# Rope attention on one core: q, k and their projections as three products of rounded operands and rests

## The chip, the cores and the metric

The kernel runs on one core of one Trainium2 chip. The metric is the device time in microseconds of one execution. Before the change it is 2147.18 us, the median of three runs (2139.17 to 2151.58).

## The reference

A stack of four layers works on 2048 tokens of 128 channels; each layer is an attention (or a recurrence) and a feed-forward part, each followed by a norm. Two places matter here. Both are causal attentions with rotary embedding over 4 sequences of 512 tokens:

- the attention of layer 2: 8 heads of 128 channels (the scores are q·k of 128 terms),
- the attention inside the feed-forward part of layer 2: 16 heads of 64 channels, with biases on q, k and v.

For each head: q = x·Wq, k = x·Wk, both rotated (`even*cos - odd*sin`, `even*sin + odd*cos`), scores = q·k with a causal mask, a softmax over the keys, the product with v, and the output projection, summed over the heads. All of it is float32.

## The kernel before

Both attentions are built by one function, `rope_attention`. The first call is named a2 (`heads=1`; in the profile its tiles begin with `a_`), the second h2 (`heads=2`; tiles begin with `h_`). Activations lie with channels on the 128 partitions and tokens along the free dimension.

The work is cut into 32 units U: 4 sequences b times 8 groups g. A unit of a2 is one head of 128 channels, a unit of h2 two heads of 64 channels, which lie on the upper and lower 64 partitions (`rows`). Each unit has four steps n = 0 to 3, one for each tile of 128 queries, in the order of query tiles 3, 0, 2, 1; a step's scores are as wide as its keys reach, so the four steps are 512, 128, 384 and 256 columns wide. In this document S512, S128, S384 and S256 are the score products of these steps (line 1210), T0 to T3 the transposes of the steps' probabilities (line 1220).

Each engine runs its own program, written out by hand, in order, and the engines wait for each other by semaphores.

- TensorE: at step K it issues the scores of step K+1, then the transposes of step K, with other work in slots between: the projections of q and k (lines 1167 and 1175) for unit U+2 in step 0, that of v in step 1 (h2 alone), the products with v for unit U-1 (line 1238) in steps 1 and 2, the output projection of unit U-1 (line 1261) in step 3. In order of time a unit reads: S128, T0, q and k projections, S384, T1, v product, S256, T2, spread sums, v products, S512 of the next unit, T3, output projection. The first scores of a unit wait for `qk_ready`, that is for both q and k of it to be rotated.
- ScalarE: exponentials (line 1324), half of the copies of transposed probabilities (line 1334), the copies of the projections out of PSUM into `raw` (line 1314, in step 0), and one copy of the sums (line 1341).
- VectorE: the row maxima (line 1387), the other copies (line 1396), the products of `raw` with the cosines (line 1365, in step 1; in h2 for q alone), in h2 the copy of v with its bias (line 1373), and in step 2 the normalisation of the output of unit U-1 (line 1410).
- SyncE: after `raw` is ready, DMAs that swap the halves of the head (line 1122).
- GpSimd: the product of the swapped halves with the sines (line 1145, q then k), in h2 the product of k with the cosines (line 1143), and the sum that is the rotated q or k (line 1150), written to one of three buffers; it waits for the scores of three units before.

Scores go to a ring of five PSUM banks, so the scores of an item wait for the copy of the item five before.

The float32 products appear in the trace as two matmul records each. The expert layers of this kernel already use the other form: there an operand is rounded to the type fp32r (hi), the rest is the operand less the rounded value (lo), and a product is hi·hi + lo·hi + hi·lo, three records (lines 661 to 663); ScalarE makes the rounded value by a copy (line 717), VectorE or GpSimd the rest by a subtraction (lines 740 and 629).

Of the kernel before, what the change touches and what calls it, by code (L numbers as in the profile page):

```python
# [16 lines left out]
P = 128  # L17
B = 4
# [7 lines left out]
def cols(c, n=T):  # L26

    return bass.ds(c * n, n)
# [1008 lines left out]
def rope_attention(core, name, *, x, heads, w_dram, table_dram=None, tables=None, theta_dram=None, v_bias_dram=None, o_bias_dram=None):  # L1037
# [34 lines left out]
    with Stage(core, name) as st:  # L1072
        w = st.sb("w", [P, G, w_cols])
        if tables is None:
# [1 line left out]
        v_bias = st.sb("v_bias", [P, G * P]) if biased else None  # L1076
        o_bias = st.sb("o_bias", [P, 1]) if biased else None
        raw, swapped, rot = (st.sb(n, [P, 2, T]) for n in ("raw", "swapped", "rot"))
        qs, ks = (st.sb(n, [P, 3, T]) for n in "qk")
        vs = st.sb("v", [P, 4, QT, P])  # L1080
        wvo = st.sb("wvo", [P, G, P]) if merged else None
        probs = st.sb("probs", [P, 4, T])
        p_t = st.sb("p_t", [P, 2, heads, QT, T])
        nmax = st.sb("nmax", [P, 8])
# [7 lines left out]
        (tables_loaded, proj_ready, v_psum, v_ready, prep_psum, prep_done, sin_ready, qk_ready, s_ready, max_ready, probs_ready,  # L1092
         pt_psum, copied_dve, copied_act, rinv_ready, wide_ready, r_psum, r_copied, values_done, y_ready, out_done, sum_done) = (st.sem(n) for n in (
             "tables_loaded", "proj_ready", "v_psum", "v_ready", "prep_psum", "prep_done", "sin_ready", "qk_ready", "s_ready",
             "max_ready", "probs_ready", "pt_psum", "copied_dve", "copied_act", "rinv_ready", "wide_ready", "r_psum", "r_copied", "values_done", "y_ready",
             "out_done", "sum_done"))
        ring = [core.psum[:, k, :] for k in range(RING)]
# [7 lines left out]
        with nc.Block() as block:  # L1105
            @block.sync
            def _(sp):
                sp.dma_start(w[:, 0, :], w_dram[0]).then_inc(w_loaded[0], 16)
                if table_dram is not None:
                    sp.dma_start(tables[:], table_dram).then_inc(tables_loaded, 16)  # L1110
                if biased:
                    sp.dma_start(v_bias[:], v_bias_dram.partition_broadcast(P)).then_inc(tables_loaded, 16)
                    sp.dma_start(o_bias[:], o_bias_dram).then_inc(tables_loaded, 16)
                for g in range(1, G):
                    sp.dma_start(w[:, g, :], w_dram[g]).then_inc(w_loaded[g], 16)
                for V in range(NU):
                    for j in range(2):
                        sp.wait_ge(raw_ready[j], V + 1)
                        if V >= 1:
                            sp.wait_ge(qk_ready, 2 * V - 1 + j)  # L1120
                        for lo, hi in halves:
                            sp.dma_start(swapped[hi:hi + half, j, :], raw[lo:lo + half, j, :]).then_inc(swap_loaded[j], 16)

            @block.gpsimd
            def _(pool):
                def widen(U):
                    pool.wait_ge(rinv_ready, U + 1)
                    if U >= 1:
                        pool.wait_ge(r_psum, U)
                    nc.gpsimd.tensor_copy(rinv_wide[:].rearrange("p (n d) -> p n d", d=dv),  # L1130
                                          rinv[:, U % 2, :, :].rearrange("p q h -> p (q h)").unsqueeze(2).to_broadcast([P, per_unit, dv])).then_inc(wide_ready, 1)

                if table_dram is not None:
                    pool.wait_ge(tables_loaded, 16)
                for V in range(NU):
                    if V > AHEAD:
                        widen(V - AHEAD - 1)
                    for j, to in enumerate((qs, ks)):
                        if j == 1 and not merged:
                            pool.wait_ge(raw_ready[1], V + 1)  # L1140
                            if V >= 1:
                                pool.wait_ge(qk_ready, 2 * V)
# [12 lines left out]
            def _(pe):  # L1155
                def project_q(V):

                    b, g = V // G, V % G
                    if V < G:
                        pe.wait_ge(w_loaded[g], 16)  # L1160
                    if V >= 4:
                        pe.wait_ge(r_copied, V - 3)
                    elif V >= 1 and merged:
                        pe.wait_ge(raw_ready[0], V)
                    elif V >= 1:
                        pe.wait_ge(v_ready, V)
                    nc.tensor.matmul(misc[0], w[:, g, 0:P], x[:, cols(b)], start=True, stop=True).then_inc(proj_ready, 1)

                def project_k(V):
                    b, g = V // G, V % G  # L1170
                    if V >= 4:
                        pe.wait_ge(y_ready, V - 3)
                    elif V >= 1:
                        pe.wait_ge(raw_ready[1], V)
                    nc.tensor.matmul(misc[1], w[:, g, qk_cols:qk_cols + P], x[:, cols(b)], start=True, stop=True).then_inc(proj_ready, 1)

                def project_v(V):

# [20 lines left out]
                def scores(K):  # L1199
                    U, q = K // QT, order[K % QT]  # L1200
                    if K % QT == 0:
                        pe.wait_ge(qk_ready, 2 * U + 2)
                    for j, h in step_items(K):
                        if j >= RING:
                            pe.wait_ge(copied_dve if copy_on_dve[j - RING] else copied_act, copy_count(j - RING))
                        elif merged:
                            pe.wait_ge(prep_done, 6)
                    for j, h in step_items(K):
                        rows = slice(h * dv, (h + 1) * dv)
                        nc.tensor.matmul(ring[j % RING][:, 0:(q + 1) * P], qs[rows, U % 3, q * P:(q + 1) * P], ks[rows, U % 3, 0:(q + 1) * P],  # L1210
                                         start=True, stop=False)
# [91 lines left out]
            def _(act):  # L1303
# [33 lines left out]
                def copy_sums(U):  # L1337
# [2 lines left out]
                        act.wait_ge(y_ready, U)  # L1340
                    nc.scalar.activation(r_sb[:], misc[0], ACT.Copy).then_inc(r_copied, 1)

                for V in range(AHEAD):
                    unrotated(V, 0)
                    unrotated(V, 1)
                exponential(0)
                for K in range(steps):
                    U, n = K // QT, K % QT
# [11 lines left out]
            def _(dve):  # L1360
                def cosine(V, j):
                    dve.wait_ge(raw_ready[j], V + 1)
                    if V >= 1:
                        dve.wait_ge(qk_ready, 2 * V - 1 + j)
# [47 lines left out]
                def add_out(b):  # L1412
# [3 lines left out]
                    else:  # L1416
                        nc.vector.tensor_tensor(core.sum[:, cols(b)], acc, x[:, cols(b)], ALU.add).then_inc(sum_done, 1)

                dve.wait_ge(tables_loaded, 32 if biased else 16)
                for V in range(AHEAD):  # L1420
                    cosine(V, 0)
# [3 lines left out]
                        copy_v(V)  # L1425
                if merged:
                    prepare()
                maximum(0)
                for K in range(steps):
                    U, n = K // QT, K % QT  # L1430
# [7 lines left out]
                    if n == 1 and U + AHEAD < NU:  # L1438
# [876 lines left out]
```

## Time and profile before

| | us |
|---|---|
| median of three runs | 2147.18 |
| the profiled execution, its own time | 2146.02 |
| its span, first to last instruction | 2144.0 |
| TensorE busy | 1754.6 (82%) |
| VectorE busy | 1277.5 (60%) |
| ScalarE busy | 1137.6 (53%) |
| GpSimd busy | 781.5 (36%) |

The times of the parts below come from the one profiled execution, in us from the start of its span. The scores of a2 run from 728.9 to about 1030, those of h2 from 1089.8 to about 1510. TensorE's granted clock is a share of 2.4 GHz. A matmul's end is modelled in the profile, so records of neighbouring matmuls overlap: what one costs is read from start to start.

### The profile page before, as it was taken

To read this page: it belongs to the slowest core of one execution; us is meant where nothing else is said; L and a number is where in the kernel's file an instruction comes from. 1 tells how busy PE (TensorE), PEld (TensorE's weight loads), DVE (VectorE), ACT (ScalarE), POOL (GpSimd) and SP (SyncE) were. 2 spreads that over 40 slices of the span, in tenths; PEclk is the share of its full clock that TensorE was granted. 3 is DMA by queue.
4 is the path that set the end of the run, shared out by engine and by line. 5 is a ranking of instruction groups with operands and counts; after the bars stand their busy time and mean duration, and the time that the engine had idled before them with its cause. 6 is when DMAs were issued, how large, how long until landed. Compare 5 with 4: busy or idle time off the path is not lost. (4 is left out here: it accounts for less than half of the span.)

```text
span 2144.0 us, 27933 instructions
## 1 busy us (share of the span) xinstructions
PE 1754.6 (82%) x8600; PEld 1034.5 (48%) x8600; DVE 1277.5 (60%) x2390; ACT 1137.6 (53%) x2332; POOL 781.5 (36%) x652
## 2 busy tenths in 40 slices
PE   5559779954999699999479999999599994657897
PEld 3337422223887355555245555554367761222664
DVE  5839575437887355555345555555469983632696
ACT  3225454433787355555445555555368873544575
POOL 1214210020453356655045555554135540001473
PEclk9869866666999899999889999999789997869799
DMA  1007100001210322222021111111055520000320
GB/s 31 1 24 173 26 1 1 1 20 54 81 68 20 98 56 53 60 60 50 17 82 42 41 42 42 41 40 31 12 208 193 197 104 17 0 7 18 108 103 20
DMA packets 52778, 120.26 MB, mean 56 GB/s; under 512 B 12724, under 2 KB 21660, under 8 KB 45468
## 3 DMA queue, kind: packets, MB, share of 16 engines
q1 hardware_dynamic: 52636, 118.55, 18.8%
q8 instruction: 66, 1.08, 0.2%
q14 instruction: 76, 0.62, 0.1%
HBM read 82.86 MB, written 2.10 MB: 40 GB/s over the span
## 5 line engine op out<-in xcount | busy, mean ns | idle before, releaser
L740 DVE TENSOR_TENSOR e_lo<-e_act,e_hi 128x512 fp32r<-128x512 f32 x200 | 213.1, 1087 | 35.7 <-ACT e_act L705 34.6
L1324 ACT ACTIVATE h_probs<-psum,h_nmax 128x512 f32<-128x512 f32 (+3 forms) x256 | 132.8, 523 | 138.5 <-DVE h_nmax L1387 83.9
L1387 DVE TENSOR_REDUCE h_nmax<-psum 128x1 f32<-128x512 f32 (+3 forms) x256 | 113.9, 487 | 130.0 <-PE psum L1213 129.7
L661 PE MATMUL psum<-f_x_hi,f_w_hi 128*128 128x512 f32 x400 | 160.4, 401 | 36.1 <-PEq L833 36.1
L680 PE MATMUL psum<-e_lo,f_w_hi 128*128 128x512 f32 x364 | 153.7, 422 | 12.5 <-DVE e_lo L740 9.2
L662 PE MATMUL psum<-f_x_hi,f_w_lo 128*128 128x512 f32 x400 | 159.4, 398 | 0.0
L663 PE MATMUL psum<-f_x_lo,f_w_hi 128*128 128x512 f32 x400 | 159.3, 398 | 0.0
L1145 POOL TENSOR_TENSOR h_swapped<-h_swapped,a2f_tables 128x512 f32<-128x512 f32 x64 | 81.7, 1276 | 203.4 <-DMA h_swapped<-h_raw 203.4
L705 ACT ACTIVATE e_act<-psum,f_b 128x512 f32<-128x512 f32 x200 | 137.7, 688 | 18.9 <-PE psum L663 14.7
L677 PE MATMUL psum<-e_hi,f_w_hi 128*128 128x512 f32 x364 | 142.6, 392 | 1.5 <-ACT e_hi L717 1.4
L678 PE MATMUL psum<-e_hi,f_w_lo 128*128 128x512 f32 x364 | 141.9, 390 | 0.0
L623 POOL TENSOR_TENSOR sum_fm<-e_part,sum_fm 128x512 f32<-128x512 f32 x60 | 99.8, 1665 | 108.8 <-DVE e_part L766 77.9
L629 POOL TENSOR_TENSOR e_lo<-e_gated,e_hi 128x512 fp32r<-128x512 f32 x50 | 73.6, 1473 | 171.4 <-ACT e_hi L717 171.4
L1324 ACT ACTIVATE a_probs<-psum,a_nmax 128x512 f32<-128x512 f32 (+3 forms) x128 | 67.5, 528 | 118.3 <-DVE a_nmax L1387 69.8
L754 DVE TENSOR_TENSOR e_gated<-e_act,e_gate 128x512 f32<-128x512 f32 x128 | 116.6, 911 | 18.5 <-ACT e_act L705 18.4
L1145 POOL TENSOR_TENSOR a_swapped<-a_swapped,a_tables 128x512 f32<-128x512 f32 x64 | 81.9, 1279 | 119.9 <-DMA a_swapped<-a_raw 119.8
L1210 PE MATMUL psum<-h_k,h_q 64*128 64x384 f32 (+3 forms) x512 | 104.9, 485 | 20.8 <-DVE h_p_t L1396 16.5
L717 ACT ACTIVATE e_hi<-e_gated 128x512 fp32r<-128x512 f32 x164 | 103.2, 629 | 27.4 <-DVE e_gated L754 20.9
L705 ACT ACTIVATE e_act<-psum 128x512 f32<-128x512 f32 x164 | 97.6, 595 | 29.2 <-PE psum L663 29.2
L1387 DVE TENSOR_REDUCE a_nmax<-psum 128x1 f32<-128x512 f32 (+3 forms) x128 | 62.6, 490 | 78.5 <-PE psum L1213 77.2
L1220 PE MATMUL psum<-ident,h_probs 128*128 128x128 f32 x640 | 108.7, 278 | 0.4 <-ACT h_probs L1324 0.4
L661 PEld LDWEIGHTS psum<-f_x_hi,f_w_hi 128*128 128x128 f32 x400 | 77.2, 193 | 51.0 <-issue 38.7
(394 smaller groups left out, 4188.4 us busy)
## 6 DMA issues: line engine op xcount, KB each, us to landing
e_gate<-gates SPq DMA_DIRECT2D x46, 1024.0 KB, 4.7
a_swapped<-a_raw SPq DMA_DIRECT2D x128, 128.0 KB, 2.3
h_swapped<-h_raw SPq DMA_DIRECT2D x256, 64.0 KB, 2.0
e_gate<-gates SPq DMA_DIRECT2D x16, 512.0 KB, 6.8
f_w<-in_l_experts SPq DMA_DIRECT2D x8, 512.0 KB, 5.6
f_w<-in_l_experts SPq DMA_DIRECT2D x32, 128.0 KB, 4.7
e_gate<-gates SPq DMA_DIRECT2D x12, 256.0 KB, 4.1
f_w<-in_l_experts SPq DMA_DIRECT2D x9, 256.0 KB, 4.9
```

The source lines that it names most:

```text
L661: nc.tensor.matmul(to, w_h, ex.x_hi[:, cols(b)], start=True, stop=False, skip_group_check=True)
L662: nc.tensor.matmul(to, w_l, ex.x_hi[:, cols(b)], start=False, stop=False, skip_group_check=True)
L663: nc.tensor.matmul(to, w_h, ex.x_lo[:, cols(b)], start=False, stop=True, skip_group_check=True).then_inc(hid_ready, 1)
L677: nc.tensor.matmul(to, w_h, hi[:, n % PLACES, :], start=start, stop=False, skip_group_check=True)
L678: nc.tensor.matmul(to, w_l, hi[:, n % PLACES, :], start=False, stop=False, skip_group_check=True)
L680: nc.tensor.matmul(to, w_h, lo[:, n % PLACES, :], start=False, stop=True, skip_group_check=True).then_inc(out_done, 1)
L705: nc.scalar.activation(act_sb[:, n % PLACES, :], hid[(n % hid_sets) * up], ex.act_func, **bias(n)).then_inc(act_ready, 1)
L740: nc.vector.tensor_tensor(lo[:, n % PLACES, :], whole, hi[:, n % PLACES, :].bitcast(F32), ALU.subtract).then_inc(lo_dve, 1)
L754: nc.vector.tensor_tensor(gated[:, n % PLACES, :], src, gate[:, s % ring, cols(b)], ALU.mult).then_inc(gated_ready, 1)
L1145: nc.gpsimd.tensor_tensor(swapped[:, j, :], swapped[:, j, :], tables[:, 2 * j + 1, :], ALU.mult).then_inc(sin_ready, 1)
L1324: nc.scalar.activation(probs[:, j % 4, 0:(q + 1) * P], ring[j % RING][:, 0:(q + 1) * P], ACT.Exp, bias=nmax[:, j % 8:j % 8 + 1], accum_out ...
L1387: nc.vector.tensor_reduce(nmax[:, j % 8:j % 8 + 1], ring[j % RING][:, 0:(q + 1) * P], AX.X, ALU.max, negate=True).then_inc(max_ready, 1)
```

## The change

In `rope_attention` alone:

- q and k of a unit, once rotated, go to two float32 buffers (three before). ScalarE copies each into an fp32r buffer, `q_hi` and `k_hi` (`round_qk`), VectorE subtracts that from the float32 value into `q_lo` and `k_lo` (`low_qk`). Three buffers each. For unit U+1 ScalarE rounds q in step 0 of unit U and k in step 1; VectorE takes the rest of q in step 1, after the cosines, and that of k in step 2, after the maximum and the copy and ahead of the normalisation.
- The scores become three products: hi·hi, lo·hi, hi·lo; in h2 each of the three is issued for both heads before the next.
- The projections of q and k become three products too, from rounded weights and rounded x and their rests. Weights and x of the first sequence and of the first three groups are split at the start; the other five groups' weights one per unit in step 1 of units 0 to 4, the other three sequences' x in step 1 of units 1 to 3.
- The first scores of a unit wait for `qk_split` (the rests of q and k), the first projections for `w_split` and `x_split`; GpSimd's sum waits for the rest of two units before instead of for the scores of three before.

```diff
-        qs, ks = (st.sb(n, [P, 3, T]) for n in "qk")
+        qs, ks = (st.sb(n, [P, 2, T]) for n in "qk")
+        q_hi, q_lo, k_hi, k_lo = (st.sb(n, [P, 3, T], F32R) for n in ("q_hi", "q_lo", "k_hi", "k_lo"))
...
# GpSimd
-                        if V >= 3:
-                            pool.wait_ge(s_ready, per_unit * (V - 2))
-                        nc.gpsimd.tensor_tensor(to[:, V % 3, :], rot[:, j, :], swapped[:, j, :], ALU.add).then_inc(qk_ready, 1)
+                        if V >= 2:
+                            pool.wait_ge(qk_split, 2 * (V - 2) + j + 1)
+                        nc.gpsimd.tensor_tensor(to[:, V % 2, :], rot[:, j, :], swapped[:, j, :], ALU.add).then_inc(rotated, 1)
...
# TensorE: the projection of q (that of k likewise)
-                        pe.wait_ge(w_loaded[g], 16)
+                        pe.wait_ge(w_split, g + 1)
+                    if g == 0:
+                        pe.wait_ge(x_split, b + 1)
...
-                    nc.tensor.matmul(misc[0], w[:, g, 0:P], x[:, cols(b)], start=True, stop=True).then_inc(proj_ready, 1)
+                    nc.tensor.matmul(misc[0], w_hi[:, g, 0, :], x_hi[:, cols(b)], start=True, stop=False)
+                    nc.tensor.matmul(misc[0], w_lo[:, g, 0, :], x_hi[:, cols(b)], start=False, stop=False)
+                    nc.tensor.matmul(misc[0], w_hi[:, g, 0, :], x_lo[:, cols(b)], start=False, stop=True).then_inc(proj_ready, 1)
...
# TensorE: the scores
-                        pe.wait_ge(qk_ready, 2 * U + 2)
+                        pe.wait_ge(qk_split, 2 * U + 2)
...
+                    for n, (q_part, k_part) in enumerate(((q_hi, k_hi), (q_lo, k_hi), (q_hi, k_lo))):
+                        for j, h in step_items(K):
+                            rows = slice(h * dv, (h + 1) * dv)
+                            nc.tensor.matmul(ring[j % RING][:, 0:(q + 1) * P], q_part[rows, U % 3, q * P:(q + 1) * P],
+                                             k_part[rows, U % 3, 0:(q + 1) * P], start=n == 0, stop=False)
...
# ScalarE
+                def round_qk(V, j):
+                    act.wait_ge(rotated, 2 * V + j + 1)
+                    if V >= 3:
+                        act.wait_ge(s_ready, per_unit * (V - 2))
+                    nc.scalar.activation((q_hi, k_hi)[j][:, V % 3, :], (qs, ks)[j][:, V % 2, :], ACT.Copy).then_inc(qk_rounded, 1)
...
+                round_x(0)
+                for g in range(AHEAD + 1):
+                    round_w(g)
...
+                    if n <= 1 and U + 1 < NU:
+                        round_qk(U + 1, n)
+                    if n == 1 and U + AHEAD + 1 < G:
+                        round_w(U + AHEAD + 1)
+                    if n == 1 and 1 <= U < B:
+                        round_x(U)
...
# VectorE
+                def low_qk(V, j):
+                    dve.wait_ge(qk_rounded, 2 * V + j + 1)
+                    nc.vector.tensor_tensor((q_lo, k_lo)[j][:, V % 3, :], (qs, ks)[j][:, V % 2, :], (q_hi, k_hi)[j][:, V % 3, :].bitcast(F32),
+                                            ALU.subtract).then_inc(qk_split, 1)
...
+                low_x(0)
+                for g in range(AHEAD + 1):
+                    low_w(g)
...
+                    if 1 <= n <= 2 and U + 1 < NU:
+                        low_qk(U + 1, n - 1)
+                    if n == 1 and U + AHEAD + 1 < G:
+                        low_w(U + AHEAD + 1)
+                    if n == 1 and 1 <= U < B:
+                        low_x(U)
```

## Rows read from the trace of the kernel before

**Rows 1.** Busy time by stretch, steady a2 and h2; columns: stretch, length, engines' busy us.
```profile
core 0: us, PE busy (x) PEld busy (x) DVE busy (x) ACT busy (x) POOL busy (x), PEclk, DMA share, GB/s
840.00:980.00 140.00, 137.17 (x603) 82.10 (x602) 72.71 (x155) 71.84 (x196) 84.57 (x75) 1.00 0.26 58
1280.00:1450.00 170.00, 164.23 (x1007) 86.05 (x1006) 94.20 (x207) 98.99 (x295) 88.74 (x78) 1.00 0.17 41
```

**Rows 2.** Timeline of one unit of a2, TensorE; columns: start us, length us.
```profile
845.02 0.39 PE L1210 MATMUL psum<-a_k,a_q 128*128 128x128 f32 x2
...
845.65 0.66 PE L1220 MATMUL psum<-ident,a_probs 128*128 128x128 f32 x4 [0.20 <-ACT a_probs L1324]
...
846.15 1.02 PE L1167 MATMUL psum<-x_fm,a_w 128*128 128x512 f32 x2
...
847.87 0.81 PE L1210 MATMUL psum<-a_k,a_q 128*128 128x384 f32 x2
...
849.68 0.59 PE L1210 MATMUL psum<-a_k,a_q 128*128 128x256 f32 x2
...
852.24 1.02 PE L1210 MATMUL psum<-a_k,a_q 128*128 128x512 f32 x2
...
854.96 0.66 PE L1220 MATMUL psum<-ident,a_probs 128*128 128x128 f32 x4 [0.20 <-ACT a_probs L1324]
```

**Rows 3.** Timeline of the same unit, the other engines.
```profile
847.21 0.60 ACT L1314 ACTIVATE a_raw<-psum 128x512 f32<-128x512 f32 x1 [0.93 <-PE psum L1167]
...
848.77 0.56 DVE L1387 TENSOR_REDUCE a_nmax<-psum 128x1 f32<-128x384 f32 x1 [1.64 <-PE psum L1213]
...
849.44 1.28 DVE L1365 TENSOR_TENSOR a_rot<-a_raw,a_tables 128x512 f32<-128x512 f32 x2
...
850.64 0.42 DVE L1387 TENSOR_REDUCE a_nmax<-psum 128x1 f32<-128x256 f32 x1
850.76 1.26 POOL L1145 TENSOR_TENSOR a_swapped<-a_swapped,a_tables 128x512 f32<-128x512 f32 x1 [2.96 <-DMA a_swapped<-a_raw]
...
853.36 0.69 DVE L1387 TENSOR_REDUCE a_nmax<-psum 128x1 f32<-128x512 f32 x1
...
854.13 0.69 ACT L1324 ACTIVATE a_probs<-psum,a_nmax 128x512 f32<-128x512 f32 x1 [1.60 <-issue]
```

**Rows 4.** Timeline of the first unit of a2: VectorE and GpSimd at once.
```profile
738.89 2.36 DVE L1365 TENSOR_TENSOR a_rot<-a_raw,a_tables 128x512 f32<-128x512 f32 x2
739.08 1.61 POOL L1145 TENSOR_TENSOR a_swapped<-a_swapped,a_tables 128x512 f32<-128x512 f32 x1 [8.40 <-DMA a_swapped<-a_raw]
```

**Rows 5.** Timeline of the expert layer of layer 2, products and splits in fp32r.
```profile
1599.77 0.68 DVE L740 TENSOR_TENSOR e_lo<-e_gated,e_hi 128x512 fp32r<-128x512 f32 x1
...
1599.88 0.63 ACT L717 ACTIVATE e_hi<-e_gated 128x512 fp32r<-128x512 f32 x1 [0.39 <-DVE e_gated L754]
...
1601.02 0.39 PE L661 MATMUL psum<-f_x_hi,f_w_hi 128*128 128x512 f32 x1
...
1601.25 0.39 PE L662 MATMUL psum<-f_x_hi,f_w_lo 128*128 128x512 f32 x1
```

**Rows 6.** Timeline of h2, from one unit's S512 into the next unit.
```profile
1300.69 1.13 PE L1210 MATMUL psum<-h_k,h_q 64*128 64x512 f32 x4
...
1301.76 0.28 PE L1213 MATMUL psum<-maskb,identb 128*128 128x128 bf16 x2
...
1303.23 0.41 DVE L1396 COPY h_p_t<-psum 128x256 f32<-128x256 f32 x1
...
1303.79 0.49 PE L1210 MATMUL psum<-h_k,h_q 64*128 64x128 f32 x4 [0.45 <-DVE h_p_t L1396]
...
1309.88 0.69 DVE L1373 TENSOR_TENSOR h_v<-psum,h_v_bias 128x512 f32<-128x512 f32 x1
...
1311.37 1.27 POOL L1145 TENSOR_TENSOR h_swapped<-h_swapped,a2f_tables 128x512 f32<-128x512 f32 x1 [4.92 <-DMA h_swapped<-h_raw]
```

**Rows 7.** Timeline of the start of a2: second projection and first scores.
```profile
712.64 0.58 PEld L1167 LDWEIGHTS psum<-x_fm,a_w 128*128 128x128 f32 x2 [1.13 <-DMA a_w<-in_l_heads]
...
728.94 2.04 PE L1210 MATMUL psum<-a_k,a_q 128*128 128x512 f32 x2 [10.22 <-DVE a_wvo L1379]
```

More of the change, by code:

```diff
@@ L1078, in rope_attention @@
         raw, swapped, rot = (st.sb(n, [P, 2, T]) for n in ("raw", "swapped", "rot"))
-        qs, ks = (st.sb(n, [P, 3, T]) for n in "qk")
+        qs, ks = (st.sb(n, [P, 2, T]) for n in "qk")
+        q_hi, q_lo, k_hi, k_lo = (st.sb(n, [P, 3, T], F32R) for n in ("q_hi", "q_lo", "k_hi", "k_lo"))
         vs = st.sb("v", [P, 4, QT, P])
         wvo = st.sb("wvo", [P, G, P]) if merged else None
+        w_hi, w_lo = (st.sb(f"w_{n}", [P, G, 2, P], F32R) for n in ("hi", "lo"))
+        x_hi, x_lo = (st.sb(f"x_{n}", [P, N], F32R) for n in ("hi", "lo"))
+        w_rounded, w_split, x_rounded, x_split, qk_rounded, qk_split = (st.sem(n) for n in (
+            "w_rounded", "w_split", "x_rounded", "x_split", "qk_rounded", "qk_split"))
         probs = st.sb("probs", [P, 4, T])
@@ L1091, in rope_attention @@
         cos_ready = [st.sem(f"{n}_cos_ready") for n in "qk"]
-        (tables_loaded, proj_ready, v_psum, v_ready, prep_psum, prep_done, sin_ready, qk_ready, s_ready, max_ready, probs_ready,
+        (tables_loaded, proj_ready, v_psum, v_ready, prep_psum, prep_done, sin_ready, rotated, s_ready, max_ready, probs_ready,
          pt_psum, copied_dve, copied_act, rinv_ready, wide_ready, r_psum, r_copied, values_done, y_ready, out_done, sum_done) = (st.sem(n) for n in (
-             "tables_loaded", "proj_ready", "v_psum", "v_ready", "prep_psum", "prep_done", "sin_ready", "qk_ready", "s_ready",
+             "tables_loaded", "proj_ready", "v_psum", "v_ready", "prep_psum", "prep_done", "sin_ready", "rotated", "s_ready",
              "max_ready", "probs_ready", "pt_psum", "copied_dve", "copied_act", "rinv_ready", "wide_ready", "r_psum", "r_copied", "values_done", "y_ready",
@@ L1119, in _ @@
                         if V >= 1:
-                            sp.wait_ge(qk_ready, 2 * V - 1 + j)
+                            sp.wait_ge(rotated, 2 * V - 1 + j)
                         for lo, hi in halves:
@@ L1141, in _ @@
                             if V >= 1:
-                                pool.wait_ge(qk_ready, 2 * V)
+                                pool.wait_ge(rotated, 2 * V)
                             nc.gpsimd.tensor_tensor(rot[:, 1, :], raw[:, 1, :], tables[:, 2, :], ALU.mult).then_inc(cos_ready[1], 1)
@@ L1174, in project_k @@
                         pe.wait_ge(raw_ready[1], V)
-                    nc.tensor.matmul(misc[1], w[:, g, qk_cols:qk_cols + P], x[:, cols(b)], start=True, stop=True).then_inc(proj_ready, 1)
+                    nc.tensor.matmul(misc[1], w_hi[:, g, 1, :], x_hi[:, cols(b)], start=True, stop=False)
+                    nc.tensor.matmul(misc[1], w_lo[:, g, 1, :], x_hi[:, cols(b)], start=False, stop=False)
+                    nc.tensor.matmul(misc[1], w_hi[:, g, 1, :], x_lo[:, cols(b)], start=False, stop=True).then_inc(proj_ready, 1)
                 def project_v(V):
@@ L1207, in scores @@
                             pe.wait_ge(prep_done, 6)
[L1208 to L1211, printed above, removed]
+                    for n, (q_part, k_part) in enumerate(((q_hi, k_hi), (q_lo, k_hi), (q_hi, k_lo))):
[3 more added lines that the diff above has]
+                                             k_part[rows, U % 3, 0:(q + 1) * P], start=n == 0, stop=False)
                     for j, h in step_items(K):
@@ L1341, in copy_sums, with round_w, round_x @@
                     nc.scalar.activation(r_sb[:], misc[0], ACT.Copy).then_inc(r_copied, 1)
+                def round_w(g):
+                    act.wait_ge(w_loaded[g], 16)
+                    pair = w[:, g, 0:2 * qk_cols].rearrange("p (j n) -> p j n", j=2)[:, :, 0:P]
+                    nc.scalar.activation(w_hi[:, g, :, :], pair, ACT.Copy).then_inc(w_rounded, 1)
+                def round_x(b):
+                    nc.scalar.activation(x_hi[:, cols(b)], x[:, cols(b)], ACT.Copy).then_inc(x_rounded, 1)
+                def round_qk(V, j):
[6 more added lines that the diff above has]
+                    round_w(g)
                 for V in range(AHEAD):
@@ L1345, in _ @@
                     unrotated(V, 1)
+                round_qk(0, 0)
+                round_qk(0, 1)
                 exponential(0)
@@ L1363, in cosine @@
                     if V >= 1:
-                        dve.wait_ge(qk_ready, 2 * V - 1 + j)
+                        dve.wait_ge(rotated, 2 * V - 1 + j)
                     nc.vector.tensor_tensor(rot[:, j, :], raw[:, j, :], tables[:, 2 * j, :], ALU.mult).then_inc(cos_ready[j], 1)
@@ L1417, in add_out, with low_w, low_x @@
                         nc.vector.tensor_tensor(core.sum[:, cols(b)], acc, x[:, cols(b)], ALU.add).then_inc(sum_done, 1)
+                def low_w(g):
+                    dve.wait_ge(w_rounded, g + 1)
+                    pair = w[:, g, 0:2 * qk_cols].rearrange("p (j n) -> p j n", j=2)[:, :, 0:P]
+                    nc.vector.tensor_tensor(w_lo[:, g, :, :], pair, w_hi[:, g, :, :].bitcast(F32), ALU.subtract).then_inc(w_split, 1)
+                def low_x(b):
+                    dve.wait_ge(x_rounded, b + 1)
+                    nc.vector.tensor_tensor(x_lo[:, cols(b)], x[:, cols(b)], x_hi[:, cols(b)].bitcast(F32), ALU.subtract).then_inc(x_split, 1)
+                def low_qk(V, j):
[5 more added lines that the diff above has]
+                    low_w(g)
                 dve.wait_ge(tables_loaded, 32 if biased else 16)
@@ L1427, in _ @@
                     prepare()
+                low_qk(0, 0)
+                low_qk(0, 1)
                 maximum(0)
```

## The prediction

> **What bounds the kernel now.** I read the page's busy shares first (TensorE 82%, VectorE 60%, ScalarE 53%), then the table by stretches, since the change touches two stages only. In the steady part of a2 TensorE is busy 137.17 of 140 us at the full 2.4 GHz, in h2 164.23 of 170; VectorE stands at 52% and 55%, ScalarE at 51% and 58% [rows 1]. So TensorE's instruction stream sets the pace, and a shorter product is worth something. The timeline says how regular it is: T0 of a2 comes at 845.65 and again at 854.96, a unit of 9.31 us [rows 2]; a unit of h2 is 13.22 us, read the same way. The page's chain of waits is empty, so I follow the waits by hand. The reader is to see two of them. In a2, T0 waits 0.20 us for the exponential, which hangs on the chain S512 (852.24), maximum (853.36), exponential (854.13), T0 (854.96): 2.72 us [rows 2, 3]. In h2, S128 waits 0.45 us for VectorE's copy that frees its bank, and the chain S512 (1300.69) to S128 (1303.79) is 3.10 us [rows 6]. Each unit is this chain plus a stretch from its end to the next S512 in which TensorE alone counts: 6.59 us in a2, 10.12 in h2.
>
> **The products.** A float32 product of 512 columns is two records 0.43 us apart: 0.86 us (the q projection at 846.15 and S384 at 847.87 have two such products between them: 1.72 [rows 2]). An fp32r product of 512 columns starts 0.23 us after the one before it [rows 5], so three cost 0.69: -0.17 for each projection and for S512. Narrow fp32r products do not stand in the trace. Below, they can't be shorter than their columns' share (0.173 for 384, 0.115 for 256, 0.058 for 128); above, they could cost as much per column as a float32 product, 0.64, 0.43 and 0.21 each. The nearest rows are single-record 128-column transposes, four of them 0.11 us apart (0.66 us for T0 with its 0.27 us tail [rows 2]), in which the weight load is the longer part. I take 0.173, 0.12 and 0.11, so three cost 0.52, 0.36 and 0.33: S384 -0.12, S256 -0.07, S128 +0.11.
>
> **a2, the gain if nothing else moves.** From T0 to S512: 6.59 - 0.34 (two projections) - 0.12 - 0.07 = 6.06. S512 to T0: 2.72 - 0.17 = 2.55; the longer S128 lies in T0's wait. Unit 8.61, against 9.31.
>
> **a2, what the added work does.** ScalarE gets two copies of 0.63 us a unit, VectorE two subtractions of 0.68 [rows 5]. On ScalarE they fall into idle time: rounding q follows the copies of the projections (done about 2.7 us after T0) and ends at 3.3, as the 384 maximum ends; rounding k follows the 384 exponential and is over at 4.8. If this cover were gone, the exponentials would come up to 0.63 later, and T2 with them. On VectorE they are on the path. In us after T0: the 384 maximum came at 3.12 (848.77) and now comes 0.46 earlier, at 2.66, because the products before it are shorter; the two cosines, at 3.79 before, start at 3.33 and end at 4.61 [rows 3]. The rest of q starts there and would end at 5.29. GpSimd's sine product of q came at 5.11 (850.76), 2.96 us behind the copy of q by its DMA; that copy is 0.17 earlier now, so it comes at 4.94. The two overlap, and the first unit of a2 shows what that costs [rows 4]: GpSimd's instruction begins 0.19 after VectorE's, and takes 1.61 instead of 1.27, so it got through 0.53 after VectorE's start; VectorE's second product then ends at 741.25, 0.56 after GpSimd's end at 740.69. They take turns. So the rest of q holds until 5.14, GpSimd runs from 5.14 to 6.41, the 256 maximum (0.42, reads PSUM, in nobody's way) is 5.29 to 5.71, and the rest of k, queued at 5.71, gets through at 6.41 and ends at 6.97. S512 waits for it by the new semaphore: 7.04 with 0.07 for the signal, instead of 6.06. Behind the waiting subtraction stands the normalisation, which ends before its output product is due. Unit: 7.04 + 2.55 = 9.59, +0.28; in the 27 units without further splits +7.6 us.
>
> The Trainium skill, page SBUF — State Buffer, section Who interferes with whom, says that a VectorE instruction with two SBUF inputs contends with a GpSimd instruction that reads SBUF, and that the later of the two is blocked entirely. The trace agrees, 1.61 against 1.27 us on GpSimd and 2.36 against 1.28 on VectorE. Did they share without blocking, the rest of k would end at 5.71 + 0.68, S512 start at 6.46 and the unit be 9.01, -0.30.
>
> **a2, units 0 to 4.** The rest of the weights (256 columns, estimated 0.41 from the 0.68 of 512) follows the rest of q: queued at 5.29, through at 6.41, done 6.70. GpSimd's sum has queued meanwhile and runs to 7.94; the 256 maximum ends at 7.1, the rest of k at 8.5, S512 at 8.57: unit 11.1, +1.8, in units 0 and 4. With the rest of x also queued (units 1 to 3) one more turn with GpSimd is lost: S512 at 10.4, unit 12.9, +3.6. Together 2 x 1.8 + 3 x 3.6 = +14.4.
>
> **h2.** The two heads' products lie on different partitions and overlap today: four records of 0.43 us each, 1.72 in a row, take 1.07 from S512 to the mask [rows 6]. I take it that the six fp32r records, issued head by head, overlap in the same way, so that each width saves what it does in a2. Below: perhaps 0.2 more. Above: no overlap at all, 4.2 us for the four widths with their masks' lead instead of 2.98. Per unit: -0.34 - 0.12 - 0.07 + 0.11 in TensorE's stretch and -0.17 in the chain, -0.59. On VectorE the rest of q follows the copy of v (ends 6.8 us after S128 before, 6.4 now) and ends at 7.1; GpSimd's sine product is at 7.58 before [rows 6], 7.5 now: no collision. The rest of k, after the maximum and the copy, waits for GpSimd until 8.8 and ends at 9.35; S512 is due at 9.7. So it is hidden with 0.3 us to spare: -0.59 x 32 = -18.9. In units 1 to 3 the rest of x uses that up, 1.5 us each: +4.5.
>
> **Starts.** Before the first copy of a projection ScalarE now waits for the third group's weights: the second came at 712.64 [rows 7], the third some 0.6 us later, against 711.4 for that copy today. The swap DMAs queue behind all the weights anyway, so little of that is seen; the first S512 (728.94) then waits for both rests behind VectorE's last copy, 2 x 0.68 and a turn with GpSimd. +3 us in each stage, +6 (between 2 and 10).
>
> **Sum.** +7.6 + 14.4 - 18.9 + 4.5 + 6 = +13.6 us on 2146.02 (the profiled execution, 2.0 us of it outside the span): 2159.6. That execution lies 1.2 us below the median of the runs shown. I say 2160.
>
> **Rivals.**
> - *TensorE keeps the pace in a2* (other side: faster). The rest of k is in time, at 6.0 after T0 or earlier; that needs VectorE to be 1 us earlier than I have it. Then a2 saves 0.70 x 32 = 22.4, h2 18.9, less 6: 2111. With sharing instead of turns: 9.6 + 18.9, less 6 and some 4 for the early units: 2127. For it: 97% busy TensorE. Against: the order of VectorE's program, and the turns of [rows 4]. It decides at S512 = 6.59, where the two effects on a2 cancel. Chance 0.25.
> - *GpSimd is first in a2.* My margin is 0.33 us (4.61 against 4.94). If the sine product goes first, it holds until 5.8, the rest of q ends at 6.3, GpSimd's sum holds until 7.6, the rest of k ends at 8.1, the unit is 10.75: +1.44 x 27 = 39 instead of 7.6, 2191. Chance 0.12.
> - *The heads of h2 don't overlap in fp32r.* Scores +1.2, projections -0.34, so +28 instead of -18.9: 2207. The overlap of today's four records speaks against it, that no fp32r record on 64 partitions exists leaves it open. Chance 0.13.
> - *My forecast,* 0.5, with its own range 2148 to 2175, by the early units and starts.
>
> **How the numbers follow.** A measurement here tells about 0.5% (10.7 us) from no change. Faster than that: the first rival and a little more, 0.27. Within: the near end of my own range, 0.18. Slower: 0.55. The range goes from 2111 to 2205.
>
> **What would show it.** In the trace after: a unit of a2 of 9.6 us with S512 waiting some 0.9 us for `k_lo`; the subtraction for k lasting about 1.3 us and GpSimd's sine product of q about 1.5; units 1 to 3 of a2 at 12 to 13 us; a unit of h2 of 12.6 us with no wait of S512; three projection records 0.23 apart. It is wrong if S512 of a2 follows the v products without a gap (then the first rival), if a pair of heads' records start more than 0.2 apart, or if S128's records are much over 0.11 apart.

## The result and the profile after

| | before | after |
|---|---|---|
| median, us (six runs each) | 2143.07 | 2161.76 |
| ratio, 95% interval | | 1.0081 (1.0052 to 1.0109) |
| profiled execution, us; span | 2146.02; 2144.0 | 2164.84; 2163.1 |
| TensorE busy | 1754.6 | 1733.1 |
| VectorE busy | 1277.5 | 1411.5 |
| ScalarE busy | 1137.6 | 1211.5 |

The kernel became slower by 0.8%; the median of before has moved from 2147.18 to 2143.07 with three more runs. TensorE has 21.5 us less to do and the span is 19.1 longer. The page of the kernel after already names what stands ahead of the scores:

```profile
PE 1733.1 (80%) x9109; PEld 1103.1 (51%) x9112; DVE 1411.5 (65%) x2542; ACT 1211.5 (56%) x2484; POOL 810.7 (37%) x652
...
L1150 POOL TENSOR_TENSOR h_swapped<-h_swapped,a2f_tables 128x512 f32<-128x512 f32 x64 | 83.2, 1300 | 202.4 <-DMA h_swapped<-h_raw 202.4
...
L1150 POOL TENSOR_TENSOR a_swapped<-a_swapped,a_tables 128x512 f32<-128x512 f32 x64 | 88.1, 1376 | 118.2 <-DMA a_swapped<-a_raw 108.7
...
L1222 PE MATMUL psum<-a_k_hi,a_q_hi 128*128 128x512 f32 (+3 forms) x128 | 69.9, 546 | 44.8 <-DVE a_k_lo L1467 44.8
```

In a2 TensorE sat idle 44.8 us for VectorE's rest of k, in front of S512, and GpSimd's sine products have a mean of 1376 ns (1279 before), those of h2 1300 (1276 before). By stretches, as in [rows 1] (stretch, length, busy us of PE, PEld, DVE, ACT, POOL, clock, DMA, GB/s), a2 steady, h2 steady, then a2's first units:

```profile
920.00:1060.00 140.00, 128.08 (x671) 91.04 (x671) 95.89 (x175) 82.85 (x218) 82.45 (x69) 1.00 0.23 50
1160.00:1500.00 340.00, 327.77 (x2374) 206.69 (x2373) 244.50 (x494) 234.46 (x680) 196.17 (x162) 1.00 0.18 43
745.00:760.00 15.00, 10.47 (x44) 7.85 (x44) 9.41 (x15) 6.15 (x17) 7.21 (x6) 0.77 0.16 36
```

TensorE's share in a2 fell from 98% to 91%, in h2 it stayed between 96 and 97%. Unit lengths, read as the distance of one output projection from the next, are 9.31 and 13.22 us before, and after (without the last three, which are shorter in both kernels):

```
a2: 13.61 14.22 12.29, then 9.45 to 9.86 (median 9.66)
h2: 12.76 12.79, then 12.59 to 12.60
```

The first output projection lies in unit 1, so this way of reading leaves out what comes before it. From the S512 of one unit to that of the next, the first five units are:

| unit | 0 | 1 | 2 | 3 | 4 |
|---|---|---|---|---|---|
| a2 before | 10.98 | 9.95 | 9.31 | 9.31 | 9.31 |
| a2 after | 14.39 | 14.65 | 12.72 | 15.12 | 12.29 |
| h2 before | 12.55 | 13.22 | 13.22 | 13.22 | 13.22 |
| h2 after | 14.06 | 14.94 | 12.76 | 12.78 | 12.60 |

Below, the lengths of units that are named by number are read from S512 to S512, all others by output projections.

One steady unit of a2 after, from T0 to the next T0, with VectorE and GpSimd from the maximum of S384 on (against [rows 2, 3]):

```profile
900.47 0.65 PE L1232 MATMUL psum<-ident,a_probs 128*128 128x128 f32 x4 [0.21 <-ACT a_probs L1336]
...
903.16 0.56 DVE L1424 TENSOR_REDUCE a_nmax<-psum 128x1 f32<-128x384 f32 x1 [1.22 <-PE psum L1225]
...
903.83 1.28 DVE L1402 TENSOR_TENSOR a_rot<-a_raw,a_tables 128x512 f32<-128x512 f32 x2
...
905.03 0.69 DVE L1467 TENSOR_TENSOR a_q_lo<-a_q,a_q_hi 128x512 fp32r<-128x512 f32 x1
...
905.37 1.47 POOL L1150 TENSOR_TENSOR a_swapped<-a_swapped,a_tables 128x512 f32<-128x512 f32 x1 [2.76 <-DMA a_swapped<-a_raw]
905.63 0.42 DVE L1424 TENSOR_REDUCE a_nmax<-psum 128x1 f32<-128x256 f32 x1
905.97 1.43 DVE L1467 TENSOR_TENSOR a_k_lo<-a_k,a_k_hi 128x512 fp32r<-128x512 f32 x1
...
907.45 0.51 PE L1222 MATMUL psum<-a_k_hi,a_q_hi 128*128 128x512 f32 x1 [0.63 <-DVE a_k_lo L1467]
...
910.14 0.66 PE L1232 MATMUL psum<-ident,a_probs 128*128 128x128 f32 x4 [0.21 <-ACT a_probs L1336]
```

The reader is to see the two turns. The sine product (POOL, 905.37) arrives 0.34 us after the rest of q began and takes 1.47 instead of 1.27; the rest of k arrives during it and takes 1.43 instead of 0.68. S512 waits for that and starts 6.98 us after T0; the next T0 comes 2.69 after it. In h2 the same stretch from the 256 maximum on (x2 is both heads):

```profile
1300.84 0.68 DVE L1467 TENSOR_TENSOR h_q_lo<-h_q,h_q_hi 128x512 fp32r<-128x512 f32 x1
...
1302.04 1.27 POOL L1150 TENSOR_TENSOR h_swapped<-h_swapped,a2f_tables 128x512 f32<-128x512 f32 x1 [4.79 <-DMA h_swapped<-h_raw]
...
1302.57 1.29 DVE L1467 TENSOR_TENSOR h_k_lo<-h_k,h_k_hi 128x512 fp32r<-128x512 f32 x1
...
1304.19 0.51 PE L1222 MATMUL psum<-h_k_hi,h_q_hi 64*128 64x512 f32 x2
1304.53 0.40 PE L1222 MATMUL psum<-h_k_hi,h_q_lo 64*128 64x512 f32 x2
1304.77 0.40 PE L1222 MATMUL psum<-h_k_lo,h_q_hi 64*128 64x512 f32 x2
...
1307.13 0.33 PE L1222 MATMUL psum<-h_k_hi,h_q_hi 64*128 64x128 f32 x2 [0.45 <-DVE h_p_t L1433]
```

There the rest of q is over before GpSimd starts; the rest of k waits its turn too (1.29), ends at 1303.86 and S512 follows at 1304.19 with no wait. S128 comes 2.94 after S512, 3.10 before [rows 6].

The 19.1 us of span, by parts of the two traces (from the first S512 of a stage to its last output projection, and what lies between):

| part | before | after | difference | forecast |
|---|---|---|---|---|
| up to a2's first weights DMA | 706.5 | 708.0 | +1.5 | 0 |
| start of a2 | 22.4 | 24.2 | +1.8 | +3 |
| units of a2 | 302.1 | 331.1 | +29.0 | +22.0 |
| between | 38.3 | 37.9 | -0.3 | 0 |
| start of h2 | 20.5 | 22.4 | +1.9 | +3 |
| units of h2 | 424.7 | 410.1 | -14.5 | -14.4 |
| rest | 629.5 | 629.3 | -0.2 | 0 |

### The profile page after: what moved, and what is told of

It reads as the page before. It is cut to its first block and busy times, and to the rows that moved or that the text cites. A ratio compares the mean times of both kernels' runs of the same rounds, so it can differ in the third digit from the quotient of the medians.

```text
span 2163.1 us, 29382 instructions
## 1 busy us (share of the span) xinstructions
PE 1733.1 (80%) x9109; PEld 1103.1 (51%) x9112; DVE 1411.5 (65%) x2542; ACT 1211.5 (56%) x2484; POOL 810.7 (37%) x652
## 3 DMA queue, kind: packets, MB, share of 16 engines
q1 hardware_dynamic: 52636, 118.55, 18.8%
## 5 line engine op out<-in xcount | busy, mean ns | idle before, releaser
L680 PE MATMUL psum<-e_lo,f_w_hi 128*128 128x512 f32 x364 | 153.9, 423 | 12.3 <-DVE e_lo L740 9.0
L1150 POOL TENSOR_TENSOR a_swapped<-a_swapped,a_tables 128x512 f32<-128x512 f32 x64 | 88.1, 1376 | 118.2 <-DMA a_swapped<-a_raw 108.7
L1222 PE MATMUL psum<-a_k_hi,a_q_hi 128*128 128x512 f32 (+3 forms) x128 | 69.9, 546 | 44.8 <-DVE a_k_lo L1467 44.8
```

The costliest lines, as they stand in the source:

```text
L680: nc.tensor.matmul(to, w_h, lo[:, n % PLACES, :], start=False, stop=True, skip_group_check=True).then_inc(out_done, 1)
```

## Experiments

All times are medians in us; each ratio is to the kernel before, run beside it on the same chip.

**The two halves.** One kernel keeps the old function for a2, the other for h2:

```diff
-    rope_attention(core, "a2", ...)
+    rope_attention_plain(core, "a2", ...)      # h2_only; a2_only does so for "h2"
```

> Leaves the attention of layer 2 (a2) as it was before; only the attention inside the feed-forward part (h2) has the three products. My account: the whole loss is a2's, h2's unit is 12.60 us instead of 13.22 and its start and first units give some 7 us back, so the time is about 12 to 13 us under the kernel before (0.994, about 2131). Rival, that h2 gains only because a2 before it leaves the clock or the queues in another state: unit above 12.8 and ratio 1.00.

> The other half: only a2 has the three products. My account: unit of 9.65 us and slow first units, +32 us over the kernel before (1.015, about 2176), so that the two halves add up to the whole change (+19). Rival, that the halves act on each other: their sum is off by more than 5 us.

Measured: h2 alone 2126.63, ratio 0.9929 (0.9905 to 0.9953); a2 alone 2176.52, ratio 1.0147 (1.0124 to 1.0170), a2's units 9.65 with 14.18, 14.16 and 11.75 first. The two sum to +0.76%, the whole change gave +0.81%: no effect of one half on the other shows, and the loss is a2's alone. Both rivals fell.

**GpSimd waits for the rest of k.** Were VectorE's work late by its place in the queue or by the turns?

```diff
...
+                        if merged and j == 0 and V >= 2:
+                            pool.wait_ge(qk_split, 2 * (V - 1) + 2)
                         pool.wait_ge(swap_loaded[j], (V + 1) * (16 * len(halves)))
```

> In a2 GpSimd begins the sine product of q only when VectorE has finished the rest of k of that unit, so the two subtractions meet nothing on GpSimd. If taking turns with GpSimd is what makes the rest of k late, that instruction falls from 1.43 to 0.68 us, S512 comes 0.6 to 0.7 earlier and the unit goes from 9.65 to about 9.0; with the first units shorter too (10 instead of 12 to 14 us) the time is some 25 us below the changed kernel, 0.996 of the kernel before. Rival, that the subtractions are late by their place in VectorE's queue alone: unit stays at 9.6. Second rival, that GpSimd, 1.1 us later, itself becomes late for the next unit: unit 9.6 or more with waits for GpSimd.

Measured: 2138.53, ratio 0.9983 (0.9968 to 0.9998), 23 us under the changed kernel; a2's first units 10.27, 10.25 and 9.66, the others 9.33. The trace of a unit, VectorE, ScalarE and TensorE:

```profile
904.14 0.42 DVE L1426 TENSOR_REDUCE a_nmax<-psum 128x1 f32<-128x256 f32 x1
904.48 0.68 DVE L1469 TENSOR_TENSOR a_k_lo<-a_k,a_k_hi 128x512 fp32r<-128x512 f32 x1
...
905.21 0.50 PE L1224 MATMUL psum<-a_k_hi,a_q_hi 128*128 128x512 f32 x1
905.43 0.60 ACT L1355 ACTIVATE a_r_sb<-psum 128x512 f32<-128x512 f32 x1
...
906.12 0.69 DVE L1449 TENSOR_TENSOR a_y<-psum,a_r_sb 128x512 f32<-128x512 f32 x1 [0.96 <-PE psum L1252]
...
906.72 0.68 DVE L1426 TENSOR_REDUCE a_nmax<-psum 128x1 f32<-128x512 f32 x1
...
906.96 1.10 PE L1275 MATMUL psum<-a_y,a_wvo 128*128 128x512 f32 x2 [0.47 <-DVE a_y L1449]
...
908.32 0.66 PE L1234 MATMUL psum<-ident,a_probs 128*128 128x128 f32 x4
```

All 32 rests of k now take 0.68 to 0.69 us (1.42 in the median of the kernel after), by a change that touches GpSimd's start alone: the turns are shown. The first five units show it too, with all the splits of weights and x still ahead of the rest of k: 11.48 and 11.11 for units 0 and 1 instead of 14.39 and 14.65, and 52.8 us for the five instead of 69.2. S512 still follows the rest of k by 0.05 us, but it comes 6.21 us after T0 instead of 6.98. The unit is 9.33, not 9.0: a new chain took over. The rest of q still stands ahead of the 256 maximum, so the exponential and the copies behind it on ScalarE are late, the copy of the sums ends at 906.03, the normalisation starts at 906.12, and the 512 maximum, whose last score record started at 906.03 and ended about 906.3, stands behind it until 906.72. T0 comes 3.11 us after S512 instead of 2.69.

**The rest of q one step earlier.** On top of that, in a2:

```diff
# ScalarE
+                    if n == 0 and U + 1 < NU and merged:
+                        round_qk(U + 1, 0)          # ahead of the copies of the projections
...
-                    if n <= 1 and U + 1 < NU:
+                    if (n == 1 or n == 0 and not merged) and U + 1 < NU:
                         round_qk(U + 1, n)
...
# VectorE
+                    if n == 0 and U + 1 < NU and merged:
+                        low_qk(U + 1, 0)            # after the reciprocals, no longer after the cosines
...
-                    if 1 <= n <= 2 and U + 1 < NU:
+                    if (n == 2 or n == 1 and not merged) and U + 1 < NU:
                         low_qk(U + 1, n - 1)
```

> On top of the run in which GpSimd waits: in a2 ScalarE rounds q ahead of the copies of the projections and VectorE takes the rest of q in step 0, so that the 256 maximum follows the cosines directly. There the unit was 9.33, since the 256 maximum, the exponential and copies behind it, the copy of the sums and so the normalisation were 0.7 us late, and the 512 maximum stood behind the normalisation. If that is the cause, T0 comes 2.6 us after S512 instead of 3.1 and the unit is 8.7, TensorE alone setting it: about 2120 us, 0.989. Rival, that the 512 exponential is late by ScalarE's own work: unit stays near 9.3. Second rival, that GpSimd, which starts the sine product 5.7 us after T0, is late for the rounding of k: waits of ScalarE for the rotated k, unit above 9.

Measured: 2124.03, ratio 0.9915 (0.9899 to 0.9931), a2's unit 8.76:

```profile
909.41 0.42 DVE L1428 TENSOR_REDUCE a_nmax<-psum 128x1 f32<-128x256 f32 x1
909.74 0.68 DVE L1471 TENSOR_TENSOR a_k_lo<-a_k,a_k_hi 128x512 fp32r<-128x512 f32 x1
...
910.98 0.48 PE L1224 MATMUL psum<-a_k_hi,a_q_hi 128*128 128x512 f32 x1
...
911.38 0.69 DVE L1451 TENSOR_TENSOR a_y<-psum,a_r_sb 128x512 f32<-128x512 f32 x1 [0.96 <-PE psum L1252]
...
912.03 0.69 DVE L1428 TENSOR_REDUCE a_nmax<-psum 128x1 f32<-128x512 f32 x1
...
913.63 0.66 PE L1234 MATMUL psum<-ident,a_probs 128*128 128x128 f32 x4
```

The rest of k is ready 0.6 us before S512 is due, T0 comes 2.65 after S512, and the unit is close to the 8.61 that the prediction gave for TensorE alone. Both rivals fell. A turn is still lost in each unit, elsewhere: the rest of q now meets GpSimd's sum for k and takes 1.28 us in the median instead of 0.69, but what stands behind it there, the 384 maximum, does not hold TensorE up: S512 follows 6.11 us after T0, where 6.06 was reckoned for TensorE alone. The unit now saves 0.55 us against before, with the same products and the same splits as the slower kernel. Its time can't be told from that of h2 alone: the intervals overlap.

**The first units.** The remaining splits go to step 3:

```diff
-                    if n == 1 and U + AHEAD + 1 < G:
+                    if n == 3 and U + AHEAD + 1 < G:
                         low_w(U + AHEAD + 1)
-                    if n == 1 and 1 <= U < B:
+                    if n == 3 and 1 <= U < B:
                         low_x(U)
...
# round_w and round_x on ScalarE likewise
```

> The splits of the remaining weights and x move from step 1 to step 3 of the same units, behind the rest of k. My account, that the first units of a2 (13.6, 14.2 and 12.3 us) are long because two more turns with GpSimd stand ahead of the rest of k: they fall to 9.7 to 10.5, h2's to 12.6 to 12.8, the time to 11 us under the changed kernel, 1.003 of the kernel before. Rival, that the low granted clock of the start (0.77) is what makes them long: at most 3 us are gained and the clock stays at 0.77.

Measured: 2157.27, ratio 1.0067 (1.0047 to 1.0086): 4.5 us less than the changed kernel, where 11 were expected. a2's first units are 10.43, 10.59, 10.60, 10.55 instead of 13.61, 14.22, 12.29, 9.64: 7.6 us less. Units 0 and 1 stay long, 13.14 and 13.53. The granted clock of 745 to 760 us was 0.77 in the kernel after, where TensorE was busy 10.47 of these 15 us, and is 0.86 here with 12.66 busy; where GpSimd waits it is 0.90 with 13.49, in the kernel before 1.00 with 14.82. So the low clock went with TensorE's waiting, and it did not stay at 0.77, as the rival had it. h2's first units, which I had said would stay, are 13.55 to 13.76 instead of 12.79 and less, and give back some 4 us; in step 3 the splits stand ahead of the next maxima there, but that this is the cause was not tried. The kernel after shows the loss that was removed, VectorE and GpSimd taking turns through the unit that also splits weights and x:

```profile
755.93 1.67 POOL L1150 TENSOR_TENSOR a_swapped<-a_swapped,a_tables 128x512 f32<-128x512 f32 x1 [3.33 <-DMA a_swapped<-a_raw]
756.39 1.49 DVE L1459 TENSOR_TENSOR a_w_lo<-a_w,a_w_hi 128x256 fp32r<-128x256 f32 x1
757.68 1.32 POOL L1155 TENSOR_TENSOR a_q<-a_rot,a_swapped 128x512 f32<-128x512 f32 x1
757.81 1.74 DVE L1463 TENSOR_TENSOR a_x_lo<-x_fm,a_x_hi 128x512 fp32r<-128x512 f32 x1
758.97 1.71 POOL L1150 TENSOR_TENSOR a_swapped<-a_swapped,a_tables 128x512 f32<-128x512 f32 x1
...
759.81 1.41 DVE L1467 TENSOR_TENSOR a_k_lo<-a_k,a_k_hi 128x512 fp32r<-128x512 f32 x1
...
761.27 0.51 PE L1222 MATMUL psum<-a_k_hi,a_q_hi 128*128 128x512 f32 x1 [3.68 <-DVE a_k_lo L1467]
```

**The projections left in float32.** All `w_hi`, `w_lo`, `x_hi`, `x_lo` work goes:

```diff
-                    nc.tensor.matmul(misc[0], w_hi[:, g, 0, :], x_hi[:, cols(b)], start=True, stop=False)
-                    nc.tensor.matmul(misc[0], w_lo[:, g, 0, :], x_hi[:, cols(b)], start=False, stop=False)
-                    nc.tensor.matmul(misc[0], w_hi[:, g, 0, :], x_lo[:, cols(b)], start=False, stop=True).then_inc(proj_ready, 1)
+                    nc.tensor.matmul(misc[0], w[:, g, 0:P], x[:, cols(b)], start=True, stop=True).then_inc(proj_ready, 1)
...
```

> The projections stay float32 products, without the splits of weights and x; scores as in the changed kernel. My account: the first units of a2 lose their excess (13 us) and the starts some 4, h2's unit rises by 0.34 to 12.94, a2's by about 0.3 to 9.95 since the cosines, and with them the turns, shift: about 2159, nearly the changed kernel's time. Rival, that the projections' split costs more than it gives also in steady units: a2's unit falls below 9.65.

> The early rest of q and GpSimd's wait, with float32 projections: a2's unit 9.0, h2's 12.94, no slow first units: 2127 us, 0.993. If the split projections' start and first units cost more than the 0.68 us a pair of units they save, this one is the faster of the two kernels with the early rest of q.

Measured: scores alone 2166.11, ratio 1.0110 (1.0094 to 1.0126), a2's units 9.97 to 10.01 from unit 2 on, but for one of 10.27, h2's 12.90. With the early rest of q 2140.06, ratio 1.0002 (0.9989 to 1.0015), units 9.10 and 12.90. The steady units came out as said (9.95, 12.94; 9.0, 12.94), the times are 7 and 13 us above what they were said to be. Part of that stands in the traces, for two expectations fell. Units 0 and 1 of a2 did not lose their excess with the splits of weights and x: with scores alone they are 15.46 and 13.59, together as long as in the kernel after. And the starts gave nothing back: from the first weights DMA to the first S512 it takes 25.5 us in a2 and 21.8 in h2 with scores alone, 26.8 and 21.1 with the early rest of q, against 24.2 and 22.4 in the kernel after. The second one's profiled execution took 2133.33, the lowest of twelve, and it began a2 9 us sooner than that of the kernel before, in code that is the same. Its starts and units of a2 and h2 come to 5 us less than before, its median to no difference; these 5 us were not seen in a trace. Against the kernel with split projections and the same early rest (2124.03) it is slower by some 0.9% by the two ratios: the split projections are worth keeping once the rests are out of the way. While the rests are in it, what they are worth (1.0110 against 1.0081) does not stand clear of the intervals.

**The heads in turn.** In h2 the three products of one head, then those of the other:

```diff
-                    for n, (q_part, k_part) in enumerate(((q_hi, k_hi), (q_lo, k_hi), (q_hi, k_lo))):
-                        for j, h in step_items(K):
+                    for j, h in step_items(K):
+                        for n, (q_part, k_part) in enumerate(((q_hi, k_hi), (q_lo, k_hi), (q_hi, k_lo))):
```

> h2 issues all three products of one head, then the three of the other. If the engine keeps the order of issue, the heads overlap only where one ends and the next begins, and the unit rises from 12.60 by 0.9 to 1.2 us (time +30 to +38, about 2195). Rival, that TensorE runs the two heads side by side whatever the order of issue: unit 12.6 and no change.

Measured: 2157.57, ratio 1.0068 (1.0044 to 1.0091), h2's unit 12.60, as in the kernel after. My expectation fell, the rival holds. S512 of a unit in this kernel, both heads' records side by side (x2; the two start 0.01 us apart) though the program issues three and three:

```profile
1304.81 0.50 PE L1222 MATMUL psum<-h_k_hi,h_q_hi 64*128 64x512 f32 x2
1305.14 0.40 PE L1222 MATMUL psum<-h_k_hi,h_q_lo 64*128 64x512 f32 x2
1305.37 0.40 PE L1222 MATMUL psum<-h_k_lo,h_q_hi 64*128 64x512 f32 x2
```

Unit 1 of h2 took 18.49 in this trace instead of 14.94. There the rests of w and x met GpSimd's products and took 1.50 and 1.76 us: the same turns as in a2.

**The starts.** On top of the early rest of q, each group's weights are split between the copies of the projections:

```diff
-                for g in range(AHEAD + 1):
-                    round_w(g)
+                round_w(0)
                 for V in range(AHEAD):
                     unrotated(V, 0)
                     unrotated(V, 1)
+                    round_w(V + 1)
...
# low_w on VectorE likewise
```

> On top of the run with the early rest of q: at the start each group's weights are split just before the projection that needs them, between the copies of the projections, instead of three groups ahead of the first copy. If the wait for the third group's weights is part of what the starts cost (S512 of a2 first at 732.2 against 728.9, the first output of h2 5 us later after a2's last), both starts give some 2 to 3 us back: about 2119. Rival, that the starts are bound by the swap DMAs behind the weight loads and by the two rests after the last copy: no change, 2124.

Measured: 2127.39, ratio 0.9940 (0.9916 to 0.9963). From the first weights DMA to the first S512 it takes 26.2 us in a2 and 21.2 in h2, against 25.0 and 21.5 with the early rest of q alone: nothing gained, the expectation fell. The traces bear out the rival. The first weights DMA is issued at 702.3 in both. The first copy of a projection then begins at 707.64 instead of 709.46, but GpSimd's first sine product, which waits for the swap DMA, begins at 714.90 instead of 714.21. And at the end of the start stand the two rests, here in the kernel after:

```profile
729.28 1.27 DVE L1416 COPY a_wvo<-psum 128x512 f32<-128x512 f32 x2
...
730.47 1.10 DVE L1467 TENSOR_TENSOR a_q_lo<-a_q,a_q_hi 128x512 fp32r<-128x512 f32 x1
731.50 0.68 DVE L1467 TENSOR_TENSOR a_k_lo<-a_k,a_k_hi 128x512 fp32r<-128x512 f32 x1
732.23 0.80 PE L1222 MATMUL psum<-a_k_hi,a_q_hi 128*128 128x512 f32 x1 [11.35 <-DVE a_k_lo L1467]
```

From the end of the last copy (730.55) to S512 it is 1.7 us; before it was 0.15 (`a_wvo` ended at 728.79, S512 at 728.94 [rows 7]). The start of a2 became 1.8 us longer, most of it by these two rests. In h2 S512 waited for GpSimd's rotated k before; now the rounding of k and its rest stand behind that (0.63 and 1.07 us), of 1.9 us that the start became longer.

## Why the prediction was right

2160 was forecast and 2161.76 measured; by its own working, +13.6 on the profiled execution against +18.8 (2164.84 less 2146.02). So the mechanism held and the difference was put 5 us too low; that the time itself is met within 2 us is partly luck, since the median of before fell by 4 us with more runs.

- *The products.* Three projection records lie 0.23 us apart, S384's 0.17 to 0.18, S256's 0.12, S128's 0.11: the values taken for the widths of which before had no row. The upper bounds (as much per column as float32) were far off. TensorE's path from T0 to S512 in a2, 6.06 in the prediction, was bared by the early rest of q: 910.98 - 904.87 = 6.11.
- *The turns in a2.* Forecast: the sine product about 1.5 us, the rest of k about 1.3, S512 7.04 after T0; measured 1.47, 1.43 and 6.98. The unit was 9.66, not 9.59: the chain from S512 to T0 was 2.69 instead of 2.55. The first of the three S512 records is followed after 0.34 instead of the 0.23 taken; that is 0.1 of it (0.31 where S512 follows the v products at once, with the early rest of q). The Trainium skill, page SBUF — State Buffer, section Who interferes with whom, says that a VectorE instruction with two SBUF inputs contends with a GpSimd instruction that reads SBUF. This case's runs agree from both sides: 1.42 us with GpSimd at work and 0.68 without. It also says that the order of issue decides who waits, and the sine product (1.47, behind the rest of q) and the rest of k (1.43, behind the sine product) show that in one unit.
- *Units 0 to 4 of a2.* +14.4 was forecast, +20.3 measured, of the +29.0 of all units; the 25 steady ones behind them lost 0.35 each, 8.9. The term was undersized by 6 us. The working put 1.8 on units 0 and 4 and 3.6 on units 1 to 3; measured are 3.4 and 3.0, and 4.7, 3.4 and 5.8. The working took the full clock, and over these five units the granted clock was 0.74, 0.79 and 0.87 (732.2 to 746.6, to 761.3, to 801.4 us). It also put units 0 and 1 down to the splits of weights and x, but without these they are as long (15.46 and 13.59), and with GpSimd held back they are 11.48 and 11.11. So most of their excess comes with the turns of the two rests; how much of the 6 us is the clock, no run separates.
- *h2.* -14.4 forecast, -14.5 measured; the unit 12.63 against 12.60. The rest of k was hidden with 0.33 us to spare (0.3 forecast). A steady unit saved 0.62 instead of 0.59 (13.22 less 12.60). But the term of +4.5 for units 1 to 3 was right in size and wrong in its reason. The rest of x was to use up the spare time there, 1.5 us each; units 2 and 3 are only 0.17 longer than the steady ones. The excess over the steady saving, 4.8 us, lies almost whole in units 0 and 1, which became 1.5 and 1.7 us longer than before, and with float32 projections, where no x is split, they are longer still (14.57 and 15.28). From 1138 to 1153 us, in unit 1, the granted clock was 0.77; in unit 1 of the kernel before, 1102 to 1116 us, it was 1.00. The cause was not tried. That the sum fits is luck.
- *Starts.* +6 forecast, +3.7 measured. The mechanism, two rests behind VectorE's last copy and a turn, is what the trace of a2 shows; in h2 it is the rounding and the rest of k behind GpSimd's sum. The size was 2.3 too high.
- *The rivals.* TensorE keeping the pace was not what happened, but it is what a2 does once GpSimd waits and the rest of q is moved, and then with most of the gain that it named: 0.55 of 0.70 us. GpSimd was not first: the sine product came 0.34 after the rest of q, as the margin of 0.33 said. The heads overlap, in either order of issue.
- *What the prediction passed over:* the second chain, over the 256 maximum, the copy of the sums and the normalisation, that holds the unit at 9.33 as soon as the turns are gone. Its bound for that case, 9.01, was too low by 0.3.

## What to carry to other kernels

Before work is moved onto an engine that is half idle, write down when in the unit it would run and what waits behind it; a 0.7 us instruction cost 0.35 us a unit where it stood, and with the same work in another place and GpSimd held back the unit gained 0.55. Here a VectorE subtraction with two operands in SBUF took twice as long where GpSimd was at work on SBUF (1.42 against 0.68 us), so place the two by time, not by load, and if they must meet, let them meet where nothing stands behind. And when one such wait is taken away, look for the next chain at once: here it was worth another 14 us.

## What the runs showed of the hardware

- Two products on different halves of the partitions run side by side even where each half's three products stand in a row in the program: pairs of records at 1304.81, 1305.14 and 1305.37, unit 12.60 in both orders. Here nothing was gained by interleaving them by hand.
- Narrow fp32r products of 128 rows follow each other after 0.11 us (128 columns), 0.12 (256), 0.17 to 0.18 (384) and 0.23 (512), at the full granted clock: below 256 columns a product gets hardly cheaper, and three of 128 columns (0.33) cost more than one float32 product (0.22 from S128 to its mask in the kernel before).
- Work ahead of TensorE in few units can cost more than the work: with 0.4 and 0.7 us more of VectorE's own work, units 2 to 4 of a2 took 12.3 to 15.1 us, against 9.66 in the steady ones. With the same work and GpSimd held back they took 9.7 to 10.3, so most of it was lost turns; the granted clock, 0.77 from 745 to 760 us, was 0.90 then.
